# Moving a visit of probabilities times V ahead of the blocks for the maximum, in each slot of an attention pipeline

## The reference, cut to what matters

```python
q = (h @ Wq).reshape(Bb, Ss, H, Dh)
k = (h @ Wk).reshape(Bb, Ss, H, Dh)
v = (h @ Wv).reshape(Bb, Ss, H, Dh)
scores = jnp.einsum('bqhd,bkhd->bhqk', q, k) / jnp.sqrt(jnp.float32(Dh))
attn = jax.nn.softmax(scores, axis=-1)
ctx = jnp.einsum('bhqk,bkhd->bqhd', attn, v).reshape(Bb, Ss, Dd)
```

## Time and profile before

| | |
|---|---|
| median of 3 runs | 3923.48 us (3914.27 to 3926.55) |
| span of the profiled execution | 3920.8 us; its own time is not listed apart from the runs |
| PE, TensorE matmuls | 3528.2 us busy, 90% |
| PEld, TensorE weight loads | 1918.7 us busy, 49% |
| DVE, VectorE | 2914.5 us busy, 74% |
| ACT, ScalarE | 2613.0 us busy, 67% |
| POOL, GpSimd | 696.1 us busy, 18% |

### The profile page before, as it was taken

How to read it: one execution, slowest core, us unless ns; L and a number is a source line. 1 busy time by engine, 2 the same in 40 slices (tenths; PEclk the granted TensorE clock), 3 DMA queues, 4 the chain that set the end, 5 groups by cost and what they waited for, 6 DMA issues and landing times. The chain is left out here.

```text
span 3920.8 us, 87382 instructions
## 1 busy us (share of the span) xinstructions
PE 3528.2 (90%) x29108; PEld 1918.7 (49%) x29108; DVE 2914.5 (74%) x5522; ACT 2613.0 (67%) x3037; POOL 696.1 (18%) x703
## 2 busy tenths in 40 slices
PE   8477999999999999999999999999999706999990
PEld 4243444444444444444444444444444605999980
DVE  1636999999999999999999999999996522333335
ACT  2132888888888888888888888888888103555540
POOL 0000000000000000000000000000000357888856
PEclk8595999999999999999999999999999757999995
DMA  3242010101101011010101101011000623444424
GB/s 95 81 161 51 12 25 14 24 13 26 24 13 26 13 24 25 13 24 13 26 16 21 26 12 25 14 24 25 14 12 7 204 102 126 146 136 138 142 83 133
DMA packets 158897, 206.66 MB, mean 53 GB/s; under 512 B 50064, under 2 KB 123664, under 8 KB 153232
## 3 DMA queue, kind: packets, MB, share of 16 engines
q1 hardware_dynamic: 140128, 173.78, 16.5%
q0 software_dynamic: 6336, 16.79, 1.4%
q10 hardware_dynamic: 12144, 12.06, 0.9%
HBM read 134.59 MB, written 66.85 MB: 51 GB/s over the span
## 5 line engine op out<-in xcount | busy, mean ns | idle before, releaser
L742 ACT ACTIVATE probs<-s_ps 128x1024 f32<-128x1024 f32 x2048 | 2056.1, 1026 | 408.6 <-PE s_ps L661 380.2
L776 DVE TENSOR_REDUCE unit_max<-m_ps 128x1 f32<-128x512 f32 x3584 | 2250.1, 686 | 57.1 <-PE m_ps L653 56.9
L676 PE MATMUL o_ps<-probs,v_here 128*32 128x256 f32 (+1 forms) x15360 | 1282.8, 406 | 0.5 <-ACT probs L742 0.5
L661 PE MATMUL s_ps<-q_stage,k_ring 50*128 50x512 f32 x4096 | 1024.4, 493 | 0.5
L653 PE MATMUL m_ps<-k_ring,q_stage 48*128 48x512 f32 x3840 | 963.6, 421 | 46.8 <-DMA q_stage<-qs_dram 25.9
L661 PEld LDWEIGHTS s_ps<-q_stage,k_ring 50*128 50x128 f32 x4096 | 384.2, 184 | 765.1 <-issue 646.2
L653 PEld LDWEIGHTS m_ps<-k_ring,q_stage 48*128 48x128 f32 x3840 | 619.9, 187 | 163.6 <-DVE unit_max L776 134.1
L676 PEld LDWEIGHTS o_ps<-probs,v_here 128*32 128x32 f32 x15360 | 303.2, 108 | 505.7 <-issue 502.7
L597 POOL TENSOR_TENSOR neg_max<-no_max,tile_max 128x4 f32<-128x4 f32 x127 | 25.3, 199 | 2447.9 <-DVE tile_max L791 2447.9
L1509 DVE TENSOR_TENSOR hidden_low<-h_ps,hidden_high 128x512 fp32r<-128x512 f32 x184 | 127.3, 692 | 366.4 <-ACT hidden_high L1473 366.4
L1469 ACT ACTIVATE h_ps<-h_ps,b_here 128x512 f32<-128x512 f32 x184 | 121.4, 660 | 255.4 <-PE h_ps L1406 255.4
(11 more groups left out here) (184 smaller groups left out, 2433.2 us busy)
## 6 DMA issues: line engine op xcount, KB each, us to landing
w_in<-in_W SPq DMA_DIRECT2D x46, 1024.0 KB, 4.9
q_stage<-max_turned SPq DMA_DIRECT2D x2048, 0.5 KB
q_stage<-qs_dram SPq DMA_DIRECT2D x768, 32.0 KB, 1.9
k_ring<-ks_dram SPq DMA_DIRECT2D x96, 128.0 KB, 4.3
slots_dram<-zero_rows SPq DMA_DIRECT2D x24, 512.0 KB, 6.7
rows_e<-slots_dram SPq DMA_DIRECT2D x24, 512.0 KB, 3.9
y_slots_dram<-y_out ACTq DMA_DIRECT2D x23, 512.0 KB, 4.3
qs_dram<-parts SPq DMA_DIRECT2D x16, 512.0 KB, 2.7
```

What stands on the lines that cost most here:

```text
L661: last = nc.tensor.matmul(s_ps[:, t % 2, k, :], k_ring[at:at + AROWS, par, P * t:P * t + P], q_stage[at:at + AROWS, buf * CHUNK:buf * CHUN ...
L676: last = nc.tensor.matmul(o_ps[at:at + SQ, lo:hi], v_here[:, par, first_tile(t) + 2 * k, :], probs[:, t, k, lo:hi], start=(pair == 0), sto ...
L742: nc.scalar.activation(probs[:, t, :, :], s_ps[:, t % 2, :, :], ACT.Exp).then_inc(exp_done, 1)
L776: nc.vector.tensor_reduce(unit_max[:, b, qt, 2 * j + k:2 * j + k + 1], m_ps[:, block_of(t, k) % 3, :], AX.X, ALU.max).then_inc(m_read, 1 + ...
```

## The change

In each slot the visit is issued before the blocks. The turn stays last in slot 10. Nothing else changes: the instructions, their waits and the other engines' programs are the same.

```diff
                 for t in range(UNITS):
                     scores(it, c, t)
-                    if ahead:
-                        max_pair(it, c + LEAD, t)
                     for visit, slot in enumerate(SLOTS):
                         if slot == t:
                             values(it, c, visit)
                         if slot == t + UNITS and c > 0:
                             values(it, c - 1, visit)
+                    if ahead:
+                        max_pair(it, c + LEAD, t)
                     if t == TURN_SLOT and c > 0:
                         turn_o(it, c)
```

## The result

The changed kernel takes 4086.0 us (median of 4 runs, 4084.28 to 4086.71) against 3922.9 us before (median of 4 runs). The ratio on record is 1.0427, with a 95% interval of 1.041 to 1.0444; the two medians alone give 1.0416, inside it. The forecast was 4088 us. The profiled execution has a span of 4082.5 us, 161.7 more than before.

A forecast was written before the change was run, and what follows sets the result against it. TensorE's order was taken to set the pace. Terms .61 + .61 - .26 + .35 = 1.31 us a chunk, times 125 chunks 164 us, gave 4088 us from a median of 3923.5; range 4005 to 4120.

The forecast's parts named there:

- The relu slots: Slots 1 and 3: later relu delays exp, so scores of slots 3 and 5 each stall TensorE .61 us a chunk.
- The wait of m1(3): Second block of slot 3 no longer waits for VectorE to read the ring: gain .26 us a chunk.
- Slots 9 and 10: Wait of .80 us for VectorE moves from second block of slot 10 to that of slot 9: gain zero.
- the .35: Around the turn: one more entry into each matmul kind, row-split and column-split, costs .35 us a chunk, bounds 0 and .70.
- The first rival: Slots 9 and 10 give back their wait: .67 us a chunk, 84 us, 4007 us; chance 10%.
- Plain slots: Slots whose order changes without relu or turn still take 1.24 us: cost zero, at most ±.03 a slot.
- slots 11 to 15 still take 1.25: Sign to look for in the changed kernel's trace: these slots keep their length of 1.25 us.
- The chain of the maximum: VectorE's transpose and the 16 DMAs after it move by some .6 us; over 4 us are left, so cost nothing.
- The number of chunks: Whole attention: 1.31 us a chunk times 125 chunks with every part gives 164 us.
- The second rival: After each stall VectorE is late and TensorE waits again: 1.83 us a chunk, 229 us, 4152 us; chance 8%.
- Faster: Visit covers both TensorE waits for VectorE, .26 and .80, relu costs nothing: 1.06 gained a chunk, 3791 us; chance 4%.
- no change: Rival for the whole kernel: gain and stall cancel, 3923 us; chance 4%.

The follow-up runs named there:

- The first experiment: Changed kernel with ScalarE's relu of slots 1 and 3 issued behind exp(1) and exp(3) in place of ahead of them: 3969.8 us, ratio 1.0133.
- the control: Kernel before with the same move of the relu behind exp, TensorE's old order kept: 4079.3 us, ratio 1.0413.
- split visits: Kernel before with the visits of slots 12 to 15 split by columns, half ahead of the blocks and half behind: 4104.6 us, ratio 1.047.
- Slot 10 alone: Kernel before with the visit ahead of the blocks only in slot 10: 3975.2 us, ratio 1.0141.
- one slot alone: Kernel before with the visit ahead of the blocks only in slot 13, a plain slot: 4017.0 us, ratio 1.0254.

## Why the prediction was right, by its steps

- **The relu slots, two stalls of .61 us: right, with mechanism and size.** Slots 2 to 5 together grew by .94 us; the prediction had .61 + .61 - .26 = .96. The table puts .10 of each stall into the following slot (the uncovered load of s(3) and s(5)). The first experiment removes the stalls without touching TensorE's program, and the control shows that ScalarE's order alone can make a loss of that size, by the ring and not by exp.
- **The wait of m1(3) goes: right.** Slot 3 fell from 1.509 to 1.337, which is -.26 and some .09 of that uncovered load.
- **Slots 9 and 10: right for the wait; for the .35, two errors partly cancel.** Measured with slots 11 and 12, +.38 against +.35. The wait moved to slot 9 and kept its size. But the .38 is not all change of kind. A small wait for VectorE that the prediction did not have stands at m1(11). VectorE over m(10), and PEld's two loads for m(11), in the changed kernel:

```profile
1511.29 1.29 DVE L776 TENSOR_REDUCE unit_max<-m_ps 128x1 f32<-128x512 f32 x2 [0.45 <-PE m_ps L653]
```

```profile
1512.53 0.28 PEld L653 LDWEIGHTS m_ps<-k_ring,q_stage 48*128 48x128 f32 x2 [0.41 <-issue]
```

  The read of m1(10) ends at 1512.58. A load takes .18, so the second of the two starts at 1512.63, .10 behind the first and .05 behind that end; over the 80 chunks the means are .09 and .05. That leaves about .3 of the .38 for the change of kind, near the .31 of the split visits and below the .35 of the forecast. So this term's total is right partly by luck.

  The first rival, that the wait would vanish, is refuted for the changed kernel by its trace. Slot 10 alone shows why it did not pay: VectorE has the longer work in that stretch, and a visit before the blocks leaves it idle for .43 us. The change of order without the relu costs .386 a chunk, with the same wait at m1(11) in it.
- **Plain slots at zero: right, but narrower than it sounded.** The eight slots in the last group of the table differ by .001 us in sum. The sign "slots 11 to 15 still take 1.25" did not hold for slots 11 and 12, which take 1.33 each: s(11) is alone, which the prediction itself had priced, and s(12) is held up by the late m1(11). The step's argument was that opening and closing a run cost the same. It left out that this holds only while neighbours change too: one slot alone costs 96 us.
- **The chain of the maximum at nothing: nothing in the trace speaks against it.** The transpose comes 5.40 us behind the chunk's first scores in place of 4.72, and slot 0 takes 1.27 us as before. Its cover was not taken away in a run.
- **The number of chunks.** 125 times 1.32 are 165 us. The span grew by 161.7; the attention's first scores start at 355.0 us in place of 358.0, which makes up the other 3.
- **The second rival, a stall that spreads,** did not come: slots 6 to 8 are unchanged. "Faster" needed a slack of over .57 us in front of s(3); the wait of .52 there refutes it, and with it "no change".

One line of the waits would have misled a reader who started there. Waits of PEld for VectorE, in the changed kernel:

```profile
PEld m_ps L653 <- DVE unit_max L776: 791.2, 1811, 1.2
```

Before it was 134.4 us. This looks like the whole loss and more, but in plain slots it is the idle time that used to stand in front of scores' loads as "issue" (646.2 us in the kernel before): the load that opens a run is now one of the blocks', which follow a semaphore of VectorE's. Its bracket is .41 us in both kernels, and the slot lasts as long.

## What to carry to other kernels

When two engines run fixed orders against each other, look for the instruction on the second engine that stands in front of the one the first waits for: the slack of the whole loop here was .15 us, and moving work of .57 us across it cost some .6 twice a chunk, the difference of .42 and two weight loads of some .10 each that were covered before (the first block's and scores'). Keep a producer's bursts evenly spaced over a ring; a local swap that seems to cover a wait moves it one slot on, and may leave the consumer idle meanwhile. And cost each extra alternation between row-split and column-split matmuls (some .3 us here for one more entry into each kind) when stages are reordered.

## What the runs showed that I had not expected

Taking the relu slots away made the kernel before faster by .4%, though VectorE then has 32 instructions over blocks a chunk in place of 30 and is busy for 490 of 500 us. Slot 3 drops from 1.509 to 1.236 us, while slots 2 and 4 rise by only .05 and .08. The expectation of +4 us is +.03 us a chunk, and the trace has -.155. What the expectation had too long stays open.
